# Gated cross-attention and expert layer: attention programs written out for all batches on five engines, in place of a loop on four

## The chip, the cores and the metric

One NeuronCore of a Trainium2 chip runs the whole kernel. The metric is the device time of one execution in microseconds (us); the median of several runs counts. The profile is of one more execution, taken by the hardware profiler.

## The reference

Sixteen batches of 512 tokens with 256 channels. A causal attention with 16 heads of 16 channels (queries from the normalized x, keys and values from a context; only the first 512 context rows can be seen under the causal mask) is added to x through a gate, and a layer of 8 experts, each of which picks its 128 best tokens of a batch, is added through another.

```python
q = _layernorm(x) @ Wq.T;  k = ctx @ Wk.T;  v = ctx @ Wv.T
scores = einsum('bhqd,bhkd->bhqk', q, k) * SCALE
probs = softmax(where(causal, scores, -inf))
x = x + tanh(g_xattn) * (einsum('bhqk,bhkd->bqhd', probs, v) @ Wo.T + bo)
affinity = softmax(_layernorm(x) @ gate_w.T);  gating, idx = top_k(affinity, 128)
h = silu(x_in @ w_gate.T) * (x_in @ w_up.T);  out.at[idx].add(gating * (h @ w_down.T))
x = x + tanh(g_ffn) * out
```

## The kernel before

The program has two stages. `attention` goes through the 16 batches, `experts` through the 8 experts with tokens gathered from memory. The change touches the first alone.

**Passes.** The attention stage is a software pipeline written by hand. `steps(body)` returns the list of steps of one pass. A pass b works on several batches at once: the maxima of the scores and the first score groups of batch b, the other score groups and the values of batch b - 1, the output and second norm of b - 1 and b - 2, and the loads, splits and projections of b + 1 and b + 2. There are passes from -1 to 17; those whose batch would be out of range drop these steps. Each engine (SyncE, TensorE, ScalarE, VectorE, GpSimd) walks the same list and does its own part of each step, so the order of work on each engine is the order of this table.

**Steps that matter below.** "max" (L459 on TensorE, L687 on VectorE) makes the plain scores and their row maxima. "mt" and "mt+" (L501, L585, L694) turn the maxima and write them, negated and in two bf16 parts, to `m_sb`. "mrow" (L399, SyncE) sends `m_sb` as two more rows into the stacked queries `qs`, two small transfers a group. "sc" (L476, L479) makes the score products that need those rows, and ScalarE takes their exponential (L571); "pv" (L493) multiplies with the values. "xturn" and "cturn" (L363) are SyncE's transposing transfers of the split x and context, two each; "qstack" and "kstack" (L383) load the stacked queries and keys of a group from memory, three transfers each; "yturn" (L370) transposes the attention's output. "load" (L335, L337) fetches the next batch. All these transfers are issued by SyncE, in the order of the table.

**Loop and straight code.** `rounds` writes passes -1, 0, 1 and 2 out, then puts the steps of passes 3 to 13 into one loop (`eng.Fori(3, BATCH - 2)`, line 299), and writes 14 to 17 out. SyncE, TensorE, ScalarE and GpSimd use it. VectorE uses `rounds_apart`, which writes all passes out. In the loop the pass number lies in a register, and so does every value that a step waits for:

```python
def count(b, per, k):
    return b * per + k
def wait(eng, s, value):
    if not isinstance(value, int) or value > 0:
        eng.wait_ge(s, value)
def wait_apart(eng, s, value, passed):
    wait(eng, s, value)
    if not isinstance(value, int):
        eng.sem_inc(passed, 1)
```

So a step in the loop computes its value with register operations first, and `wait_apart` makes the wait an instruction of its own that also counts up `passed`. With a constant the value stands in the instruction, and a negative one or zero leaves the wait out. Line 152 of the profile is `eng.wait_ge`, line 160 the `sem_inc`. Inside the loop the DMA addresses come from registers too.

The experts stage has a loop of its own (line 976, `Fori(1, EXPERTS // 2 - 1)`, two rounds of two experts each), unchanged.

Of the kernel before, what the change touches and what calls it, by code (L numbers as in the profile page):

```python
# [13 lines left out]
BATCH = 16  # L14
# [65 lines left out]
def steps(body):  # L80


    b = body
    order = []


    extra = {
        0: {0: [("mrow", b - 1, 3)],
            1: [("ln1+", b + 1, 0), ("yt+", b - 1, 0), ("pv", b - 1, 1, 0), ("yt", b - 1, 0)],
            2: [("xsplit", b + 1, 0)],  # L90
            3: [("mt", b - 1, 3), ("ln1+", b + 1, 1), ("xturn", b + 1), ("xsplit", b + 1, 1), ("pv", b - 1, 1, 1), ("pv", b - 1, 1, 2)],
            4: [("csplit", b + 1, 0), ("o", b - 2, 0, 0), ("o", b - 2, 0, 1), ("mt+", b - 1, 3)],
            5: [("cturn", b + 1)],
            6: [("o+", b - 2, 0), ("o", b - 2, 1, 0)],
            7: [("csplit", b + 1, 1), ("o", b - 2, 1, 1), ("pv+", b - 1, 1), ("pv", b - 1, 1, 3), ("o+", b - 2, 1)],
            9: [("yt", b - 1, 1)]},
        1: {0: [("qstack", b, 2), ("kstack", b, 2)],
            1: [("yturn", b - 1, 0), ("yt+", b - 1, 1), ("mrow", b, 0), ("ysplit", b - 1, 0)],
            2: [("mt", b, 0), ("mt+", b, 0), ("ln2", b - 2, 0)],
            3: [("ln2", b - 2, 1), ("pv", b - 1, 2, 0), ("q", b + 1, 0, 0)],  # L100
            4: [("q+", b + 1, 0), ("q", b + 1, 0, 1), ("q", b + 1, 1, 0)],
            5: [("pv", b - 1, 2, 1)],
            6: [("q", b + 1, 1, 1), ("kstack", b, 3), ("q+", b + 1, 1)],
            8: [("k", b + 1, 0, 0), ("ln2+", b - 2, 1), ("pv", b - 1, 2, 2)],
            9: [("xs", b - 2), ("ln2+", b - 2, 0), ("pv", b - 1, 2, 3)]},
        2: {1: [("pv+", b - 1, 2), ("k+", b + 1, 0), ("k", b + 1, 0, 1)],
            2: [("mt", b, 1), ("mt+", b, 1)],
            3: [("load", b + 2), ("pv", b - 1, 3, 0)],
            4: [("k", b + 1, 1, 0), ("k", b + 1, 1, 1), ("k+", b + 1, 1)],
            5: [("qstack", b, 3), ("yt", b - 1, 2), ("yt+", b - 1, 2), ("pv", b - 1, 3, 1)],  # L110
            7: [("pv", b - 1, 3, 2), ("qstore", b + 1), ("vaug", b)],
            8: [("pv+", b - 1, 3), ("mrow", b, 1), ("pv", b - 1, 3, 3), ("xt", b - 2, 0), ("xt+", b - 2, 0)],
            9: [("res", b - 1), ("xt+", b - 2, 1)],
            10: [("xt", b - 2, 1)]},
        3: {0: [("kstore", b + 1)],
            1: [("mt+", b, 2), ("yt", b - 1, 3), ("yt+", b - 1, 3), ("qstack", b + 1, 0), ("mt", b, 2)],
            3: [("ll+", b - 2), ("pv", b, 0, 0), ("ll", b - 2), ("v", b + 1, 0, 0), ("kstack", b + 1, 0)],
            4: [("v+", b + 1, 0), ("v", b + 1, 0, 1), ("ln1", b + 2, 0), ("mrow", b, 2)],
            5: [("ysplit", b - 1, 1), ("save", b - 2), ("lt", b - 2), ("yturn", b - 1, 1)],
            6: [("kstack", b + 1, 1), ("v", b + 1, 1, 0), ("lt+", b - 2)],  # L120
            8: [("v", b + 1, 1, 1), ("pv", b, 0, 1), ("v+", b + 1, 1)],
            9: [("pv+", b, 0)],
            10: [("ln1", b + 2, 1), ("pv", b, 0, 2), ("qstack", b + 1, 1), ("pv", b, 0, 3)]},
    }
    for g in range(GROUPS):
        sc = (b, g - 2) if g >= 2 else (b - 1, g + 2)
        for k in range(NMAX):
            order.append(("max", b, g, k))
            if k < NSC:
                order.append(("sc", *sc, k))  # L130
            order += extra[g].get(k, [])
    return [p for p in order if not isinstance(p[1], int) or 0 <= p[1] < BATCH]
# [30 lines left out]
def flamingo(nc, x, ctx_kv, g_xattn, g_ffn, wq, wk, wv, wo, bo, gate_w, w_gate, w_up, w_down, out):  # L163
    with ExitStack() as stack:
        def sem(name):
            return stack.enter_context(nc.semaphore(name))

        def sb(ctx, name, shape, dt):
            return ctx.enter_context(nc.sbuf_tensor(name, shape, dt))

        bank = [stack.enter_context(nc.psum_tensor(f"bank{i}", [P, 512], F32)) for i in range(8)]
        max_bank, sc_bank, pv_bank, job_bank = bank[0:3], bank[3:5], bank[5], bank[6:8]


        q_dram = nc.dram_tensor("q_parts", [BATCH, GROUPS, 3, HD * GH, T], BF16, kind="Internal").ap()
        k_dram = nc.dram_tensor("k_parts", [BATCH, GROUPS, 3, HD * GH, T], BF16, kind="Internal").ap()
        tok_dram = nc.dram_tensor("tokens", [BATCH * T, 2 * D], BF16, kind="Internal").ap()

        ident = sb(stack, "ident", [P, P], F32)
        aff = sb(stack, "aff", [P, NT, BATCH * EXPERTS], F32)  # L180
        tanh_g = sb(stack, "tanh_g", [P, 2], F32)
        passed = {n: sem(f"passed_{n}") for n in ("dve", "pool", "sp")}

        with ExitStack() as ctx:
            attention(nc, ctx, stack, sb, sem, locals())
        with ExitStack() as ctx:
            experts(nc, ctx, sb, sem, locals())


def attention(nc, ctx, stack, sb, sem, g):  # L190
# [100 lines left out]
    lmax_done, lexp_done, lsum_done, lrec_done, aff_done = (  # L291
        sem(n) for n in ("lmax_done", "lexp_done", "lsum_done", "lrec_done", "aff_done"))

    def rounds(eng, body):

        for b in (-1, 0, 1, 2):
            for p in steps(b):
                body(b, p)
        with eng.Fori(3, BATCH - 2) as b:
            for p in steps(b):  # L300
                body(b, p)
        for b in range(BATCH - 2, BATCH + 2):
            for p in steps(b):
                body(b, p)

    def rounds_apart(body):

        for b in range(-1, BATCH + 2):
            for p in steps(b):
                body(b, p)  # L310
# [15 lines left out]
    with nc.Block() as block:  # L326
        @block.sync
        def _(sp):
# [85 lines left out]
            for n in ("wq", "wk", "wv", "wo"):  # L414
                load_weights(n)
            sp.dma_start(gw_raw[:, :], g["gate_w"]).then_inc(w_loaded["gate_w"], 16)
            rounds(sp, piece)
            sp.wait_ge(x1_stored, 16 * BATCH)
            sp.wait_ge(tok_stored, 16 * BATCH)

        @block.tensor
        def _(pe):
# [19 lines left out]
            def piece(body, p):  # L442
# [106 lines left out]
                elif kind == "lt":  # L549
                    wait(pe, read["ll"], count(b, 1, 1))  # L550
                    nc.tensor.transpose(to[:, 0:P], llT[:, :], ident[:, :]).then_inc(filled[kind], 1)

            rounds(pe, piece)

        @block.scalar
        def _(act):
# [91 lines left out]
            def later(body, p):  # L648
                if p[0] == "ln1+" and isinstance(p[1], int) and p[1] == 0:
                    return  # L650
                piece(body, p)

            rounds(act, later)

        @block.vector
        def _(dve):
# [112 lines left out]
            dve.wait_ge(tanh_done, 1)  # L769
            nc.vector.tensor_scalar(bias[:, :], bo_rep[:, :], tanh_g[:, 0:1], None, ALU.mult).then_inc(bias_done, 1)  # L770

            rounds_apart(piece)

        @block.gpsimd
        def _(pool):
# [101 lines left out]
                                    base=-1 - SUB * (STACK + 1), pattern=[[0, NT], [-1, P]], channel_multiplier=SUB)\  # L877
                .then_inc(tails_made, 1)
            piece(-1, ("ln1", 0, 1))
            rounds(pool, piece)  # L880


def experts(nc, ctx, sb, sem, g):
# [369 lines left out]
```

## Time and profile before

| | |
|---|---|
| median of 3 runs | 1872.76 us (1872.36 to 1877.73) |
| the profiled execution, its own time | 1872.91 us |
| its span, first to last instruction | 1871.2 us |
| TensorE busy | 1745.9 us (93%) |
| VectorE busy | 1075.4 us (57%) |
| ScalarE busy | 932.2 us (50%) |
| GpSimd busy | 931.7 us (50%) |
| mean granted TensorE clock | 0.974 of full speed |

The 1.7 us between time and span lie around the instructions. "Busy" leaves out register, branch, semaphore and DMA-issuing instructions. A busy TensorE isn't one at its peak, since matmuls are pipelined. The attention stage fills the span up to about 770 us, then the best tokens are sorted out, and the experts fill the rest from about 850 us on.

In what follows a pass of the attention stage is cut at TensorE's first "max" product of the pass: pass 2 is 129.0 to 175.5 us, pass 3 is 175.5 to 222.7, passes 4 to 13 are 222.7 to 675.2, pass 14 is 675.2 to 722.1. PE is TensorE's matmuls, PEld its weight loads; a q behind an engine's name (PEldq, SPq) is its sequencer or its DMA issues.

### The profile page before, as it was taken

The numbers are of one execution on the slowest core, as the hardware profiler recorded it, in microseconds if no ns is written. First come the engines' busy times: TensorE is split into PE (matmuls) and PEld (weight loads), VectorE is DVE, ScalarE is ACT, GpSimd is POOL, SyncE is SP. The second block draws the span as 40 slices with busy tenths as digits, with TensorE's granted clock in tenths as the row PEclk, the third lists the DMA queues.
The fourth block names the chain that finished last, engine by engine and source line by source line (L and its number), as shares of the span: only waits on it lengthen the run. The fifth ranks groups of instructions, "written<-read, shape, count | busy, mean of one in ns | idle before, by whom it ended". The sixth has DMA issues, their size and how long they took to land.

```text
span 1871.2 us, 40632 instructions
## 1 busy us (share of the span) xinstructions
PE 1745.9 (93%) x12838; PEld 1026.6 (55%) x12902; DVE 1075.4 (57%) x3480; ACT 932.2 (50%) x1812; POOL 931.7 (50%) x1026
## 2 busy tenths in 40 slices
PE   4899999999999999818999999999899999999997
PEld 1455555555555555413656565656556565656565
DVE  3788888888888888466443434343343434343421
ACT  2467777777777776523343434343343434343332
POOL 6377788777778885551332324242323232424222
PEclk8899999999999999959999999999999999999999
DMA  6767777778777786365654545656636455555221
GB/s 168 161 172 197 191 199 194 197 197 200 199 196 193 199 199 151 86 162 147 129 103 85 104 85 105 130 78 124 106 67 112 94 96 105 86 96 82 46 32 23
DMA packets 408333, 247.85 MB, mean 132 GB/s; under 512 B 289303, under 2 KB 389759, under 8 KB 408191
## 3 DMA queue, kind: packets, MB, share of 16 engines
q1 hardware_dynamic: 383183, 212.39, 49.4%
q0 software_dynamic: 24576, 33.57, 11.2%
q8 instruction: 72, 1.18, 0.3%
q14 instruction: 70, 0.57, 0.1%
q10 hardware_dynamic: 432, 0.13, 0.0%
HBM read 118.63 MB, written 58.72 MB: 95 GB/s over the span
## 4 chain that ended last, share of the span: by engine, by line
PE 51%; DVE 3%; issue 1%; DMA 1%; ACT 0%; POOL 0%; POOLq 0%; DVEq 0%
PE bank L1108 11%; PE bank L1107 11%; PE bank L1109 11%; PE bank L1125 6%; PE bank L1123 6%; PE bank L1124 6%; DVE h L1225 0%; DVE top_at L1175 0%; DVE h L1228 0%; ACT h L1153 0%; DVE work L1178 0%; DVE top L1173 0%; DMA rows<-tokens,row_now 0%; DMA out<-y,row_now 0%; DMA tokT<-rows 0%
## 5 line engine op out<-in xcount | busy, mean ns | idle before, releaser
L1073 POOL DMA_INDIRECT out<-y,row_now x128 | 202.0, 1578 | 605.9 <-ACT y L1160 581.3
L687 DVE CUSTOM_DVE_ANT_0 masked<-bank,causal 128x128 bf16<-128x128 f32 (+3 forms) x1024 | 449.6, 485 | 62.1 <-PE bank L459 60.0
L571 ACT ACTIVATE prob<-bank 128x512 f32<-128x512 f32 x640 | 360.1, 595 | 140.4 <-PE bank L479 103.1
L1225 DVE TENSOR_TENSOR h<-bank,silu 128x512 f32<-128x512 f32 x256 | 176.4, 689 | 392.5 <-PE bank L1109 258.6
L1153 ACT ACTIVATE h<-h 128x512 bf16<-128x512 f32 x256 | 161.2, 630 | 346.2 <-DVE h L1225 324.5
L1228 DVE TENSOR_TENSOR h<-h 128x512 bf16<-128x512 f32 x256 | 177.4, 693 | 179.4 <-ACT h L1153 171.8
L1125 PE MATMUL bank<-downT,h 128*128 128x256 bf16 x1024 | 279.1, 273 | 0.0
L1124 PE MATMUL bank<-downT,h 128*128 128x256 bf16 x1024 | 279.1, 273 | 0.0
L1123 PE MATMUL bank<-downT,h 128*128 128x256 bf16 x1024 | 279.1, 273 | 0.0
L459 PE MATMUL bank<-ks,qs 96*128 96x128 bf16 (+3 forms) x1024 | 254.9, 306 | 19.2 <-DMA ks<-k_parts 10.2
L1108 PE MATMUL bank<-tokT,gateT 128*128 128x512 bf16 x511 | 194.7, 381 | 35.4 <-DMA tokT<-rows 28.9
L476 PE MATMUL bank<-qs,ks 128*128 128x128 bf16 x1024 | 200.0, 221 | 12.8 <-DMA qs<-m_sb 9.1
L1107 PE MATMUL bank<-tokT,upT 128*128 128x512 bf16 x511 | 194.6, 381 | 6.7 <-DVE h L1225 6.6
L479 PE MATMUL bank<-qs,ks 98*128 98x384 bf16 (+2 forms) x768 | 196.7, 274 | 0.0
L1108 PE MATMUL bank<-tokT,upT 128*128 128x512 bf16 x512 | 194.6, 380 | 0.1
L1109 PE MATMUL bank<-tokT,upT 128*128 128x512 bf16 x512 | 194.6, 380 | 0.0
L840 POOL TENSOR_SCALAR_AFFINE_SELECT prob<-prob 128x512 f32<-128x512 f32 x256 | 156.4, 637 | 72.7 <-ACT prob L571 72.5
L493 PE MATMUL bank<-prob,v_aug 128*32 128x512 f32 (+3 forms) x2048 | 185.8, 447 | 2.9 <-ACT yT L579 2.9
L1107 PE MATMUL bank<-tokT,gateT 128*128 128x512 bf16 x481 | 182.8, 380 | 2.5 <-ACT silu L1147 0.9
L1160 ACT ACTIVATE y<-bank,gate_now 128x256 f32<-128x256 f32 x128 | 53.7, 471 | 260.7 <-PE bank L1125 260.7
L1109 PE MATMUL bank<-tokT,gateT 128*128 128x512 bf16 x481 | 183.3, 381 | 0.1
L1060 POOL DMA_INDIRECT rows<-tokens,row_now x128 | 130.1, 1016 | 92.6 <-DVE row_now L1216 54.8
(141 smaller groups left out, 2675.4 us busy)
## 6 DMA issues: line engine op xcount, KB each, us to landing
q_parts<-q_sb SPq DMA_DIRECT2D x64, 192.0 KB, 4.5
k_parts<-k_sb SPq DMA_DIRECT2D x64, 192.0 KB, 3.8
qs<-q_parts SPq DMA_DIRECT2D x64, 192.0 KB, 3.5
ks<-k_parts SPq DMA_DIRECT2D x64, 192.0 KB, 3.1
x_t<-in_x SPq DMA_DIRECT2D x16, 512.0 KB, 4.2
ctx_t<-in_ctx SPq DMA_DIRECT2D x16, 512.0 KB, 5.5
qs<-q_parts SPq DMA_DIRECT2D x64, 128.0 KB, 3.3
ks<-k_parts SPq DMA_DIRECT2D x64, 128.0 KB, 3.0
```

Of the source, the lines that this page charges most:

```text
L459: last = nc.tensor.matmul(dst[:, h * w:(h + 1) * w], qs[0:STACK, gr, h0 + h, i * P:(i + 1) * P], ks[0:STACK, gr, h0 + h, 0:w], start=True, ...
L476: last = nc.tensor.matmul(dst[:, at:at + P], ks[:, gr, h0 + h, j * P:(j + 1) * P], qs[:, gr, h0 + h, j * P:(j + 1) * P], start=True, stop= ...
L479: last = nc.tensor.matmul(dst[:, at + P:at + PWIDTH[j]], ks[0:ROWS, gr, h0 + h, j * P:(j + 1) * P], qs[0:ROWS, gr, h0 + h, (j + 1) * P:T], ...
L571: nc.scalar.activation(prob[:, gr % 2, h0:h0 + nh, POFF[tiles[0]]:POFF[tiles[0]] + w], sc_bank[SC_BANK[k]][:, 0:nh * w].rearrange("p (h w) ...
L687: last = nc.vector.tensor_tensor_reduce(masked[:, (gr * NMAX + k) % 2, part], max_bank[max_at(gr, k)][:, part], causal[:, T - w:T], 1.0, L ...
L1073: nc.gpsimd.indirect_dma_start(out_rows, bass.IndirectOffsetOnAxis(ap=row_now[:, par, c, s:s + 1], axis=0), y[:, c % 2, s, :], None, compu ...
L1107: nc.tensor.matmul(banks[it % 2][:, :], hi, xh, start=(dh == 0), stop=False)
L1108: nc.tensor.matmul(banks[it % 2][:, :], hi, xl, start=False, stop=False)
L1109: last = nc.tensor.matmul(banks[it % 2][:, :], lo, xh, start=False, stop=(dh == NH2 - 1))
L1123: nc.tensor.matmul(to, hh, wh, start=(it == 0), stop=False)
L1124: nc.tensor.matmul(to, hh, wl, start=False, stop=False)
L1125: last = nc.tensor.matmul(to, hl, wh, start=False, stop=(it == IT - 1))
```

## The change

`rounds` loses its loop and becomes what `rounds_apart` was: passes -1 to 17 one after the other, with the pass number a constant. All five engines use it. The order of the steps in a pass is the same.

```diff
--- before.py
+++ after.py
@@ -291,19 +291,7 @@
     lmax_done, lexp_done, lsum_done, lrec_done, aff_done = (
         sem(n) for n in ("lmax_done", "lexp_done", "lsum_done", "lrec_done", "aff_done"))
 
-    def rounds(eng, body):
-
-        for b in (-1, 0, 1, 2):
-            for p in steps(b):
-                body(b, p)
-        with eng.Fori(3, BATCH - 2) as b:
-            for p in steps(b):
-                body(b, p)
-        for b in range(BATCH - 2, BATCH + 2):
-            for p in steps(b):
-                body(b, p)
-
-    def rounds_apart(body):
+    def rounds(body):
 
         for b in range(-1, BATCH + 2):
             for p in steps(b):
@@ -414,7 +402,7 @@
             for n in ("wq", "wk", "wv", "wo"):
                 load_weights(n)
             sp.dma_start(gw_raw[:, :], g["gate_w"]).then_inc(w_loaded["gate_w"], 16)
-            rounds(sp, piece)
+            rounds(piece)
             sp.wait_ge(x1_stored, 16 * BATCH)
             sp.wait_ge(tok_stored, 16 * BATCH)
 
@@ -550,7 +538,7 @@
                     wait(pe, read["ll"], count(b, 1, 1))
                     nc.tensor.transpose(to[:, 0:P], llT[:, :], ident[:, :]).then_inc(filled[kind], 1)
 
-            rounds(pe, piece)
+            rounds(piece)
 
         @block.scalar
         def _(act):
@@ -650,7 +638,7 @@
                     return
                 piece(body, p)
 
-            rounds(act, later)
+            rounds(later)
 
         @block.vector
         def _(dve):
@@ -769,7 +757,7 @@
             dve.wait_ge(tanh_done, 1)
             nc.vector.tensor_scalar(bias[:, :], bo_rep[:, :], tanh_g[:, 0:1], None, ALU.mult).then_inc(bias_done, 1)
 
-            rounds_apart(piece)
+            rounds(piece)
 
         @block.gpsimd
         def _(pool):
@@ -877,7 +865,7 @@
                                     base=-1 - SUB * (STACK + 1), pattern=[[0, NT], [-1, P]], channel_multiplier=SUB)\
                 .then_inc(tails_made, 1)
             piece(-1, ("ln1", 0, 1))
-            rounds(pool, piece)
+            rounds(piece)
 
 
 def experts(nc, ctx, sb, sem, g):
```

On TensorE, where pass 3 begins. Before, this is the start of the loop (`bank` is a PSUM bank, `qs` and `ks` the stacked queries and keys, `ISA` and `REGISTER_ALU` are register operations):

```order
L299 ISA
L152 ISA [waits stack_loaded0]
L459 MATMUL bank<-ks,qs 128x128 [waits max_read]
L459 MATMUL bank<-ks,qs 128x128 x3
L152 ISA
L152 ISA [waits mrow_loaded2]
L476 MATMUL bank<-qs,ks 128x128 [waits exp_done]
L479 MATMUL bank<-qs,ks 128x384
L459 MATMUL bank<-ks,qs 128x256 [waits max_read]
L459 MATMUL bank<-ks,qs 128x256
L152 REGISTER_ALU
```

The same place with the change:

```order
L447 MATMUL bank<-ks,qs 128x128 [waits max_read,stack_loaded0]
L447 MATMUL bank<-ks,qs 128x128 x3
L464 MATMUL bank<-qs,ks 128x128 [waits exp_done,mrow_loaded2]
L467 MATMUL bank<-qs,ks 128x384
L447 MATMUL bank<-ks,qs 128x256 [waits max_read]
L447 MATMUL bank<-ks,qs 128x256
L464 MATMUL bank<-qs,ks 128x128 [waits exp_done]
L467 MATMUL bank<-qs,ks 128x256
```

The products and their order are the same; the register operations in front of them are gone, and two waits that stood apart are now in the products they belong to. Where pass 3 ends there was a branch; now the products of pass 4 follow.

On SyncE, where pass 3 begins, the transfers on the way to the first group's maxima. Before (start of the loop; `xT` and `cT` are the transposed x and context):

```order
L299 ISA
L152 REGISTER_ALU [waits mt_read]
L399 DMA qs<-m_sb 1x16x128 [waits sc_filled]
L399 DMA qs<-m_sb 1x16x128
L152 ISA
L363 DMA_TRANSPOSE xT<-x_nat 128x8x128 [waits x_lo_split,q_filled]
L363 DMA_TRANSPOSE xT<-x_nat 128x8x128
L363 DMA_TRANSPOSE cT<-c_nat 128x8x128 [waits c_lo_split,v_filled]
L363 DMA_TRANSPOSE cT<-c_nat 128x8x128
L152 ISA
L152 ISA [waits q_stored]
L383 ISA [waits sc_filled]
```

With the change:

```order
L387 DMA qs<-m_sb 1x16x128 [waits sc_filled,mt_read]
L387 DMA qs<-m_sb 1x16x128
L351 DMA_TRANSPOSE xT<-x_nat 128x8x128 [waits q_filled,x_lo_split]
L351 DMA_TRANSPOSE xT<-x_nat 128x8x128
L351 DMA_TRANSPOSE cT<-c_nat 128x8x128 [waits v_filled,c_lo_split]
L351 DMA_TRANSPOSE cT<-c_nat 128x8x128
L371 DMA qs<-q_parts 48x2048 [waits sc_filled,q_stored]
L371 DMA qs<-q_parts 32x2048
```

The transfers stand in the same order, with no register operations between them. Lines moved up by 12 with the deleted function. As a whole TensorE's program has 8553 rows where it had 6261 (rows group instructions, and a loop's rows stand once), SyncE's 939 instead of 513, ScalarE's 1526 instead of 1058, GpSimd's 874 instead of 470, and VectorE's 3338 as before.

## Rows read from the trace of the kernel before

**Rows 1.** Page, part 1: busy us (share), instructions.

```profile
PE 1745.9 (93%) x12838; PEld 1026.6 (55%) x12902; DVE 1075.4 (57%) x3480; ACT 932.2 (50%) x1812; POOL 931.7 (50%) x1026
```

**Rows 2.** Line 299 (the passes' loop): count, ns min/median/max, first and last start.

```profile
L299 PEldq COMPARE_BRANCH  x11: 76/208/235, 222.0 to 674.5; - x11
...
L299 PEldq MOVE  x1: 29/29/29, 174.7 to 174.7; - x1
```

**Rows 3.** Stretches: us, busy (x) by engine, PEclk, DMA, GB/s; passes 2, 3, 14.

```profile
129.00:175.50 46.50, 44.79 (x426) 25.98 (x422) 39.10 (x170) 33.27 (x66) 36.25 (x47) 1.00 0.72 184
175.50:222.70 47.20, 44.97 (x426) 26.13 (x422) 39.25 (x170) 33.36 (x66) 36.05 (x47) 1.00 0.75 183
675.20:722.10 46.90, 45.04 (x426) 25.98 (x423) 38.52 (x168) 33.27 (x66) 36.35 (x47) 1.00 0.84 182
```

**Rows 4.** The same, last line: passes 4 to 13 together.

```profile
sum 452.50, PE 448.10 PEld 261.44 DVE 389.41 ACT 331.99 POOL 360.70; mean PE 44.81 PEld 26.14 DVE 38.94 ACT 33.20 POOL 36.07
```

**Rows 5.** Line 152 (waits), stretch 358.4 to 403.7, one loop pass.

```profile
L152 PEldq ALU_OP  x97: 32/32/36, 358.8 to 401.8; - x97
...
L152 PEldq EVENT_SEMAPHORE  x18: 51/51/51, 359.2 to 398.4; - x18
...
L152 PEldq FUSED_REGOPS  x17: 37/37/65, 358.9 to 403.7; - x17
```

**Rows 6.** DMA queues, passes 4 to 13: packets, MB, share.

```profile
q1 hardware_dynamic: 120661, 89.66, 79.0%
q14 instruction: 18, 0.15, 0.1%
```

**Rows 7.** DMA queues, pass 14.

```profile
q8 instruction: 4, 0.07, 0.6%
q14 instruction: 4, 0.03, 0.2%
```

**Rows 8.** DMA queues, pass 2.

```profile
q8 instruction: 3, 0.05, 0.5%
q14 instruction: 4, 0.03, 0.3%
```

**Rows 9.** Waits, pass 2: us, times, longest.

```profile
PE bank L476 <- DMA qs<-m_sb: 1.7, 1, 1.7
```

**Rows 10.** Waits, pass 3.

```profile
PE bank L476 <- DMA qs<-m_sb: 1.7, 2, 0.9
```

**Rows 11.** Waits, pass 14.

```profile
PE bank L476 <- DMA qs<-m_sb: 1.6, 1, 1.6
```

**Rows 12.** Waits, passes 4 to 13.

```profile
PE bank L476 <- DMA qs<-m_sb: 1.8, 5, 0.6
```

**Rows 13.** Timeline, SyncE issues in pass 13: start, us.

```profile
642.70 2.62 SPq L363 DMA_TRANSPOSE cT<-c_nat  x2
...
647.36 1.32 SPq L383 DMA_DIRECT2D ks<-k_parts  x3
```

**Rows 14.** The same in pass 3.

```profile
188.46 3.73 SPq L363 DMA_TRANSPOSE cT<-c_nat  x2
```

**Rows 15.** DMA queues, 189.5 to 191.2 us.

```profile
q8 instruction: 1, 0.02, 5.0%
```

**Rows 16.** The SyncE issues in pass 14.

```profile
692.24 1.97 SPq L383 DMA_DIRECT2D ks<-k_parts  x3
```

**Rows 17.** DMA queues, 692.0 to 693.5 us.

```profile
q8 instruction: 1, 0.02, 4.4%
```

**Rows 18.** Timeline, TensorE in pass 14: start, us, idle before.

```profile
700.23 0.23 PE L476 MATMUL bank<-qs,ks 128*128 128x128 bf16 x1 [1.55 <-DMA qs<-m_sb]
```

**Rows 19.** Line 976 (the experts' loop).

```profile
L976 PEldq COMPARE_BRANCH  x2: 76/3070/6063, 1340.7 to 1597.1; - x2
```

**Rows 20.** Timeline, TensorE at the experts' back edge.

```profile
1347.62 0.63 PE L1108 MATMUL bank<-tokT,gateT 128*128 128x512 bf16 x1 [4.96 <-issue]
```

## The prediction

> **What bounds the kernel now.** I read the page's busy times first: TensorE has work for 1745.9 us [rows 1] of the 1871.2 us span, far ahead of every other engine. Then I cut the attention stage into passes. Line 299 is the loop that holds passes 3 to 13 on TensorE: it is entered at 174.7, its branch runs first at 222.0 and last, the eleventh time, at 674.5 [rows 2]. Ten passes (4 to 13) thus take 452.5 us, 45.25 us each. In the stretches, TensorE is busy for 448.1 of these 452.5 us [rows 4], so only 4.4 us of gaps are left in ten passes, back edges included. A loop pass is TensorE's own work and hardly anything else. That is the first thing to see: **the loop has next to nothing to give back**.
>
> The second is that the passes that are already written out are the longer ones. Pass 2 takes 46.5 us and pass 14 takes 46.9; pass 3, the first time through the loop's code, takes 47.2. All three have the same matmuls (x426) and full clock (PEclk 1.00) [rows 3]. Against 45.25 that is 1.25, 1.65 and 1.95 us more.
>
> The third is where the excess lies. In each of the three, TensorE waits 1.6 to 1.7 us for the transfer qs<-m_sb [rows 9 to 11]; in ten loop passes together it waits 1.8 us for it [rows 12]. In pass 14 it is one hole of 1.55 us, at 700.23 [rows 18]: the first score product (L476) of a group needs the row of negated maxima. That small transfer stands in SyncE's queue behind the two cT transposes, six stack loads and one yT transpose.
>
> The fourth is what differs. The q8 and q14 instruction queues carry program code. In passes 4 to 13 there are 18 packets on q14 and none on q8 [rows 6]; in pass 14 alone there are 4 on each [rows 7], in pass 2 there are 3 and 4 [rows 8]. So TensorE, ScalarE, GpSimd and SyncE find a loop's code still at hand, and only VectorE, written out already, keeps loading (18 packets in ten passes). The size 0.07 MB over 4 is about 16 KB a block on q8, 8 KB on q14. Where such a block falls into the chain of transfers, SyncE's issues drag: the pair of cT transposes takes 2.62 us to issue in pass 13 [rows 13], and 3.73 us in pass 3 [rows 14], with one q8 block between 189.5 and 191.2 [rows 15]. The three ks loads take 1.32 us in pass 13 [rows 13] and 1.97 us in pass 14 [rows 16], with one q8 block between 692.0 and 693.5 [rows 17].
>
> **The change, part by part.**
>
> *Register arithmetic goes.* In one loop pass TensorE's sequencer runs 97 ALU_OPs of 32 ns and 17 FUSED_REGOPS of 37 ns [rows 5], 3.7 us in all, beside 45 us of matmuls that it runs ahead of. What hides it is the queue of matmuls; had it cost time, it would stand in the 4.4 us of gaps. Gain between 0 and 4.4 us over the ten passes. I take 0, since the written-out passes, which have none of it, aren't shorter. For SyncE, ScalarE and GpSimd the same: their operations of this kind end in a wait for TensorE's pace, and what they could save lies in the same 4.4 us.
>
> *Extra wait instructions go* (the waits that also count up the semaphore "passed"). Bound and value are the same 0 to 4.4 us, counted once.
>
> *Ten back edges go.* TensorE's takes 208 ns at the median [rows 2], inside the sequencer's lead. Value 0; bounds again in the 4.4 us.
>
> *Code must now be loaded in every pass.* This is the term that counts. A pass of TensorE is some 426 matmuls and 422 weight loads [rows 3] plus about 20 waits, near 870 instructions; pass 14 loaded 4 blocks for them and pass 2 loaded 3. Ten passes so add some 34 blocks on q8 and about 20 on q14. Their bytes are nothing (0.07 MB in a pass against 8 to 9 MB); it is their place that costs. The nearest rows are the three passes that do load: 1.25, 1.65 and 1.95 us. Ten passes at these prices are 12.5, 16.5 and 19.5 us. From below the bound is 0, should the blocks fall beside the chain; from above I take the dearest pass, 19.5 us, and a little over. I choose 1.3 us a pass, near the cheapest of the three, because a block comes every 13 us (45 us over 3.4) and only a part of the pass is sensitive: in pass 13, which starts at 629.9, it runs from the issue of the cT pair at 642.70 [rows 13] to about where pass 14 has its hole, 25 us after a start at 675.2 [rows 3, 18]. Some 12 us of 45, by this estimate, so some passes will be missed. **+13 us.**
>
> *Pass 3 itself* (47.2 us) already loads its code, and passes 1, 2, 14 and later are untouched. 0, within 1 us either way.
>
> *The experts stage* isn't changed, but its code moves. TensorE's back edge at line 976 holds it for up to 6063 ns [rows 19], and TensorE idles 4.96 us there [rows 20]. Where the target lies may change what that branch costs: between 5 us less and 5 us more. I take 0.
>
> The sum is made against the profiled execution: 1872.91 + 13 = **1886 us**. That execution is 0.15 us above the median of the three runs (1872.76), so it serves for both. About 0.3% (5.6 us) is what a measurement of this kernel can tell from no change.
>
> The Trainium skill, "Runtime: NRT & Kernel Launch", section "Instruction fetch mechanics", speaks against my term: it says that the sequencer fetches the next block while the current one runs, and that crossing a block is mostly hidden. By it the sum would be 1872.9. The written-out passes disagree, not because TensorE starved for code, but because other transfers came late.
>
> **The rivals.**
>
> *The loads are hidden (chance 0.18).* Then passes 2, 3 and 14 are long for reasons of their own: pass 2 stands near the start, pass 3 carries the entry into the loop, pass 14 is the first after it. For it: three passes are few. Against it: all three show the same wait of 1.6 to 1.7 us, which the ten others have at 0.18 us in the mean and 0.6 at the longest [rows 12]. Time 1872.9, or down to 1872.9 - 4.4 = 1868.5 if all gaps close too.
>
> *The loads cost more (0.13).* Not only SyncE's issues but ScalarE's or GpSimd's own code comes late, in passes whose blocks meet both the first and the second group's chain, as pass 3 (two waits [rows 10]). At 2.2 us a pass the change costs 22 us, 1895; it decides if the mean of passes 4 to 13 goes over 47.2.
>
> *Faster: the back edges were dear (0.04).* The place is TensorE's branch. If each of ten cost what the experts' one costs, 4.96 us [rows 20], the time would be 1872.9 - 49.6 = 1823. But 4.4 us of gaps in ten passes exclude nearly all of it. What is left: all gaps closed, and the experts' loop lands better, 1872.9 - 4.4 - 5.0 = 1863.5. It decides from 5.6 us on, so it needs both. The same section of the Trainium skill states this rule (a taken branch out of the resident window waits for a fetch, hence a preference for full unrolling); the trace agrees at the experts' back edge and not at this loop's, where the branch takes 208 ns.
>
> *The change doesn't do what it says* has no room here: the order of the work in a pass is the same in both programs.
>
> **How the numbers follow.** Forecast 0.65 at 1886 us. The range reaches down to the hidden case, 1873, and up to the dear one, 1895; below 1873 and above 1895 I leave about 2 in 10. Slower by over 0.3% (above 1878.5): the forecast and the dear case, 0.77, the two summing to 0.78 with a little off for a forecast that comes out small. Within 0.3%: the hidden case and that little, 0.19. Faster: 0.04.
>
> **What would show it.** Right: in passes 4 to 13 of the new profile q8 carries 3 or 4 packets a pass, about 34, and q14 some 38 in place of 18; these passes average 46 to 47 us; the waits of L476 for qs<-m_sb grow from 1.8 us to 8 or more; the line-152 ALU_OPs are gone from the attention stage; TensorE's matmul times and PEclk stay. Wrong: q8 packets in each pass and yet passes of 45.3 us (then hidden), or passes of 45.3 us with a different total (then the experts' back edge moved), or passes under 44.9 us, which would say that register work did hold TensorE up.

## The result and the profile after

| | before | with the change |
|---|---|---|
| median of 12 runs each | 1873.72 us (1872.36 to 1878.44) | 1881.07 us (1878.10 to 1885.80) |
| ratio, 95% interval | 1 | 1.0037 (1.0027 to 1.0047) |
| the profiled execution, its span | 1872.91, 1871.2 us | 1884.75, 1883.0 us |

The change makes the kernel 7 us slower, 0.37%. The profiled execution of the changed kernel is one of its slower ones, 3.7 us above the median, so the profile shows 11.8 us of difference where the medians show 7.4.

Page, part 1, of the changed kernel (compare [rows 1]):

```profile
PE 1752.6 (93%) x12838; PEld 1026.7 (55%) x12902; DVE 1075.8 (57%) x3480; ACT 934.3 (50%) x1812; POOL 933.0 (50%) x1026
```

The stretches of the changed kernel, cut into passes as before (columns as in [rows 3]): pass 3, passes 4 to 13 together, then passes 4, 9, 10 and 12 alone, and pass 14.

```profile
174.00:222.40 48.40, 46.54 (x426) 26.54 (x423) 39.16 (x170) 33.65 (x66) 36.28 (x47) 0.96 0.85 189
222.40:683.70 461.30, 451.75 (x4214) 260.98 (x4211) 390.20 (x1691) 333.22 (x660) 361.52 (x461) 0.99 0.81 195
222.40:267.30 44.90, 44.79 (x425) 25.98 (x421) 38.85 (x170) 33.25 (x66) 36.05 (x47) 1.00 0.80 193
450.50:498.60 48.10, 46.45 (x426) 26.52 (x423) 39.25 (x170) 33.55 (x66) 36.30 (x47) 0.96 0.79 185
498.60:547.30 48.70, 46.53 (x425) 26.58 (x421) 39.10 (x170) 33.63 (x66) 36.22 (x47) 0.96 0.87 190
593.50:638.50 45.00, 44.76 (x426) 25.98 (x423) 38.90 (x170) 33.23 (x66) 36.08 (x47) 1.00 0.81 199
683.70:733.90 50.20, 47.66 (x425) 26.92 (x422) 38.54 (x168) 33.76 (x66) 36.28 (x47) 0.93 0.75 169
```

Passes 4 to 13 take 461.3 us against 452.5 [rows 4], 8.8 us more. Pass 4 and pass 12 are as short as any loop pass; pass 9 and pass 10 are 3 us longer. Pass 14 was already written out and is 3.3 us longer too (50.2 against 46.9). Pass 3 is 1.2 us longer (48.4 against 47.2), and what comes ahead of it is shorter by 1.5, so pass 4 begins within 0.3 us of where it did; everything after pass 14 takes the same 1149.1 us. And another column moves: the granted clock, 1.00 in all of [rows 3], is 0.96 in passes 3, 9 and 10 and 0.93 in pass 14.

The DMA queues in passes 4 to 13 (compare [rows 6]):

```profile
q8 instruction: 34, 0.56, 0.5%
q14 instruction: 34, 0.28, 0.2%
```

34 blocks on q8 where there were none, 34 on q14 where there were 18. The waits of TensorE in the same ten passes (compare [rows 12]):

```profile
PE bank L464 <- DMA qs<-m_sb: 7.2, 8, 1.6
...
PE bank L447 <- DMA ks<-k_parts: 0.8, 2, 0.7
```

The wait of the score product for its maxima has grown from 1.8 to 7.2 us, and a wait for the stacked keys has come up. The deepest hole, in pass 14 (compare [rows 18]), with what SyncE issued ahead of it (compare [rows 16]):

```profile
709.34 0.29 PE L464 MATMUL bank<-qs,ks 128*128 128x128 bf16 x1 [2.45 <-DMA qs<-m_sb]
```

```profile
699.05 1.72 SPq L371 DMA_DIRECT2D qs<-q_parts  x3
700.87 1.30 SPq L371 DMA_DIRECT2D ks<-k_parts  x3
...
703.95 1.17 SPq L387 DMA_DIRECT2D qs<-m_sb  x2
```

The clock adds a second price to the same holes. TensorE's timeline after the hole of pass 10, and the granted clock (PEclk, third column from the right) of three short stretches there:

```profile
521.97 0.40 PE L447 MATMUL bank<-ks,qs 96*128 96x128 bf16 x4 [0.67 <-DMA ks<-k_parts]
523.82 0.23 PE L464 MATMUL bank<-qs,ks 128*128 128x128 bf16 x1 [1.45 <-DMA qs<-m_sb]
...
525.02 1.49 PE L510 MATMUL bank<-cT,wkT 128*128 128x512 bf16 x3
...
529.25 1.46 PE L510 MATMUL bank<-cT,wkT 128*128 128x512 bf16 x6
```

```profile
524.00:526.00 2.00, 2.00 (x10) 1.08 (x8) 0.78 (x4) 1.34 (x3) 1.91 (x2) 0.50 1.07 273
526.00:527.50 1.50, 1.50 (x8) 0.80 (x7) 0.33 (x1) 1.05 (x3) 1.00 (x1) 0.55 1.15 369
527.50:531.00 3.50, 3.50 (x28) 1.61 (x26) 2.27 (x10) 1.96 (x5) 1.77 (x2) 1.00 1.05 268
```

TensorE stood still for 0.67 and 1.45 us, with four products between. Then it ran at half clock (0.50, the lower of its two levels, 1.2 GHz) until about 527.3: three of the products of L510 take 1.49 us, six take 1.46 at full clock behind it. Such a stretch is 3.4 us long in passes 3, 9 and 10, at 199.7, 476.1 and 523.9 us, and 6.8 us in pass 14, at 708.2; half of it is lost. Of the 6.8 us in pass 14 the first 1.1 us still lie in the hole, in which no product runs. In passes 2 to 14 of all profiles of this study, each drop to half clock begins in a hole before score products or within about 1 us after one. That splits the 8.8 us of passes 4 to 13 into 5.4 us more waiting for m_sb (7.2 less 1.8), 0.8 us for the keys, and 3.4 us of clock (two stretches of 3.4 us, half of each): 9.6 us, a little over what is to be explained.

Register work is indeed gone. Line 152 on TensorE in pass 7 (compare [rows 5], 97 ALU_OPs and 17 FUSED_REGOPS, now none):

```profile
L152 PEldq EVENT_SEMAPHORE  x32: 51/51/51, 359.3 to 404.3; - x32
```

### The profile page after: what moved, and what is told of

Same layout as the page of the kernel before. It is cut to its first block, busy times and chain, and to the rows that moved or that the text cites. A ratio compares the mean times of both kernels' runs of the same rounds, so it can differ in the third digit from the quotient of the medians.

```text
span 1883.0 us, 37315 instructions
## 1 busy us (share of the span) xinstructions
PE 1752.6 (93%) x12838; PEld 1026.7 (55%) x12902; DVE 1075.8 (57%) x3480; ACT 934.3 (50%) x1812; POOL 933.0 (50%) x1026
## 4 chain that ended last, share of the span: by engine, by line
PE 51%; DVE 3%; DMA 1%; issue 1%; ACT 0%; POOL 0%; POOLq 0%; DVEq 0%
PE bank L1096 11%; PE bank L1095 11%; PE bank L1097 11%; PE bank L1113 6%; PE bank L1111 6%; PE bank L1112 6%; DVE h L1213 0%; DVE top_at L1163 0%; DVE h L1216 0%; ACT h L1141 0%; DVE work L1166 0%; DVE top L1161 0%; DMA rows<-tokens,row_now 0%; DMA tokT<-rows 0%; DMA out<-y,row_now 0%
```

## The experiments

Theory A: TensorE's 16 KB code blocks make SyncE's chain of transfers late. Rival B: it is the code of the three other engines, or their constants. All times are medians; "before" is the kernel before, run on the same chip in the same rounds.

### One part of the change at a time

TensorE alone written out:

```diff
-            rounds(pe, piece)
+            rounds_apart(piece)
```

> The kernel before, with TensorE's attention program alone written out; SyncE, ScalarE and GpSimd keep the loop. Theory A (TensorE's 16 KB code blocks fall into SyncE's chain of transfers and make them late): q8 carries about 33 packets in passes 4 to 13, q14 stays near 18, and most of the loss of the full change is here: 5 to 8 us over before, about 1880. Rival B (it is the code of SyncE, ScalarE and GpSimd, in 8 KB blocks, or their waits and issues in constant form): no more than 1 us over before, 1873 to 1875. If both share it: 3 to 4 us over.

Measured: 1887.91 us against 1873.46, ratio 1.0078 (1.0060 to 1.0096): **14.5 us slower, twice the full change.** Its ten passes take 465.3 us, 12.8 more than before:

```profile
q8 instruction: 34, 0.56, 0.5%
q14 instruction: 18, 0.15, 0.1%
```

```profile
PE bank L476 <- DMA qs<-m_sb: 9.7, 10, 1.6
...
PE bank L459 <- DMA ks<-k_parts: 1.7, 3, 0.9
...
PE bank L522 <- DMA xT<-x_nat: 1.0, 2, 0.7
```

The whole cost belongs to TensorE's code, as theory A has it, but the size was missed, 14.5 us for an expected 5 to 8: something else in the full change gives 7 us back. The opposite half, with TensorE alone in the loop and the others written out (`rounds_loop` is the old `rounds`):

```diff
         @block.tensor
...
-            rounds(piece)
+            rounds_loop(pe, piece)
```

> The changed kernel, with TensorE alone put back into the loop; SyncE, ScalarE, GpSimd and VectorE are written out. q8 is empty in passes 4 to 13, q14 carries about 33. Theory A: within 1.5 us of before, 1873 to 1875. Rival B: all of the loss stays, about 1880 to 1881. Together with the run before it: if A and B add, the two excesses sum to about 7 to 8 us.

Measured: 1874.75 us, ratio 1.0008 (0.9994 to 1.0022), no difference that can be told. In passes 4 to 13 (221.2 to 677.0 us) q14 carries its 34 packets and q8 none:

```profile
q14 instruction: 34, 0.28, 0.2%
PE bank L476 <- DMA qs<-m_sb: 4.1, 9, 1.7
```

So B, which wanted 1880 to 1881, is out. The 8 KB blocks are not quite free, though: TensorE's wait for m_sb grows from 1.8 to 4.1 us and these ten passes take 455.8 us, 3.3 more than before, most of it in pass 9, which takes 48.1 us with a hole of 1.66 us and 3.4 us at half clock behind it. What happens there is read in the next section. But the two halves do not add: 14.5 and 1.3 make 7.4. Writing out the three other engines gains nothing while TensorE loops and 7 us when it doesn't. SyncE's issues show what it can be. Pass 7 starts at 358.4 in the kernel before and at 358.6 in the changed one. Before:

```profile
371.23 2.61 SPq L363 DMA_TRANSPOSE cT<-c_nat  x2
374.36 1.27 SPq L383 DMA_DIRECT2D qs<-q_parts  x3
375.88 1.32 SPq L383 DMA_DIRECT2D ks<-k_parts  x3
377.48 1.25 SPq L370 DMA_TRANSPOSE ynT<-y_nat  x1
379.09 1.18 SPq L399 DMA_DIRECT2D qs<-m_sb  x2
```

With the change:

```profile
371.09 2.60 SPq L351 DMA_TRANSPOSE cT<-c_nat  x2
373.79 1.45 SPq L371 DMA_DIRECT2D qs<-q_parts  x3
375.34 1.29 SPq L371 DMA_DIRECT2D ks<-k_parts  x3
376.73 1.24 SPq L358 DMA_TRANSPOSE ynT<-y_nat  x1
378.07 1.23 SPq L387 DMA_DIRECT2D qs<-m_sb  x2
```

The issues themselves take about the same time; the gaps between them, in which the loop's SyncE computes addresses and values, are gone. From the end of the cT pair to the start of the m_sb pair it was 5.25 us (379.09 less 373.84) and is 4.38 (378.07 less 373.69). The m_sb pair starts 19.5 us into the pass instead of 20.7. Two more kernels tell whether this is what pays. SyncE written out with TensorE:

```diff
-            rounds(sp, piece)
+            rounds_apart(piece)
...
-            rounds(pe, piece)
+            rounds_apart(piece)
```

> The kernel before with TensorE and SyncE written out (and VectorE, as before); ScalarE and GpSimd keep the loop. TensorE alone written out cost 14.5 us where the full change costs 7. Theory: SyncE's constants give the difference back, since it then issues the first group's m_sb transfers about 1.1 us earlier in a pass (19.5 in place of 20.7 us): 1879 to 1883. Rival (ScalarE or GpSimd give it back, or the difference is chance): 1885 to 1889.

Measured: 1879.03 us against 1873.61, ratio 1.0031 (1.0017 to 1.0044). And its complement, TensorE, ScalarE and GpSimd written out, SyncE in the loop:

```diff
-            rounds(pe, piece)
+            rounds_apart(piece)
...
-            rounds(act, later)
+            rounds_apart(later)
...
-            rounds(pool, piece)
+            rounds_apart(piece)
```

> The complement: TensorE, ScalarE and GpSimd written out, SyncE in the loop. Theory (SyncE's constants give it back): without them the cost stays at that of TensorE alone, 1885 to 1890, and the m_sb transfers are issued at about 20.7 us of a pass or later. Rival (ScalarE or GpSimd): 1879 to 1883.

Measured: 1886.10 us, ratio 1.0065 (1.0047 to 1.0083). Both as the theory said. In passes 4 to 13 the first group's m_sb pair is issued 19.7 to 21.3 us into a pass with SyncE written out, 20.5 to 21.7 with SyncE in the loop. The waits in passes 4 to 13, first with SyncE written out, then with SyncE in the loop (the second profile is of the slowest of its six executions, 7.5 us above their median, so it overstates the difference):

```profile
PE bank L476 <- DMA qs<-m_sb: 6.1, 7, 1.4
```

```profile
PE bank L476 <- DMA qs<-m_sb: 12.9, 13, 2.0
```

It is SyncE's straight code, without the register work, that gives back more than half of what TensorE's costs (1887.91 to 1879.03). ScalarE and GpSimd matter little: with their programs written out as well, 1887.91 becomes 1886.10 and 1879.03 becomes 1881.07.

### Room in the chain

If the blocks cost only by making the m_sb transfers late, then room ahead of these transfers must take the cost away. The m_sb pair of the first group waits for nothing but its place in SyncE's queue: VectorE writes it about 5 us before SyncE issues it. In pass 13 of the kernel before, the two are (VectorE's timeline, SyncE's timeline):

```profile
645.22 0.27 DVE L694 SCALAR_TENSOR_TENSOR m_sb<-bank,m_sb 16x128 bf16<-16x128 f32 x1
```

```profile
650.57 1.18 SPq L399 DMA_DIRECT2D qs<-m_sb  x2
```

In the table of steps, "mrow" goes ahead of "yturn":

```diff
-            1: [("yturn", b - 1, 0), ("yt+", b - 1, 1), ("mrow", b, 0), ("ysplit", b - 1, 0)],
+            1: [("mrow", b, 0), ("yturn", b - 1, 0), ("yt+", b - 1, 1), ("ysplit", b - 1, 0)],
```

In the kernel before:

> The kernel before, with the first group's two small m_sb transfers (mrow) issued by SyncE ahead of the yT transpose instead of behind it, nothing else. They are issued about 1.3 us earlier, and no longer wait for that transpose to land. Theory (the chain cT, stacks, yT, m_sb ends last before the first score product): the holes of 0.2 to 0.8 us there vanish, 1 to 4 us faster than before, 1869 to 1873. Rival (the stack loads or VectorE's maxima end last there): no change.

Measured: 1868.91 us against 1873.46, ratio 0.9977 (0.9966 to 0.9988), 4.5 us faster, a little over the 1 to 4 expected. In the changed kernel:

> The changed kernel with the same one step moved (m_sb transfers ahead of the yT transpose). Theory: the loss sits in the hole before the first group's score product, which now has a microsecond or more to spare, so it recovers more than the same move does in the kernel before: 5 to 9 us faster than the changed kernel, 1872 to 1876. Rival 1 (TensorE itself waits for its code, or the loss is spread over other waits): it stays at 1879 to 1881. Rival 2 (the move only helps as much as in the kernel before): 1 to 4 us faster, 1877 to 1880.

Measured: 1872.11 us, ratio to before 0.9995 (0.9979 to 1.0010), so 9.0 us under the changed kernel's 1881.07. The same move is worth twice as much where code is loaded. The second group has the same shape one step further on: its "mrow" stands behind "qstore", four stores of 192 KB. With that pair moved as well:

```diff
-            7: [("pv", b - 1, 3, 2), ("qstore", b + 1), ("vaug", b)],
-            8: [("pv+", b - 1, 3), ("mrow", b, 1), ("pv", b - 1, 3, 3), ("xt", b - 2, 0), ("xt+", b - 2, 0)],
+            7: [("pv", b - 1, 3, 2), ("mrow", b, 1), ("qstore", b + 1), ("vaug", b)],
+            8: [("pv+", b - 1, 3), ("pv", b - 1, 3, 3), ("xt", b - 2, 0), ("xt+", b - 2, 0)],
```

> The kernel before with the first group's m_sb transfers ahead of the yT transpose, as in the run that gained 4.5 us, and the second group's ahead of the q stores too. Theory (the holes of 0.4 to 0.9 us before the second group's score product, at 34 to 36 us of a pass, come from these transfers standing behind four stores): 1 to 3 us faster than with the first move alone, 1866 to 1868. Rival (the stores are then late and hold up the next pass's stacks): 1869 to 1875.

Measured: 1862.89 us against 1873.61, ratio 0.9942 (0.9925 to 0.9958). That is 6 us beyond the first move, where 1 to 3 were expected. In passes 4 to 13 one wait of 0.2 us is left:

```profile
PE bank L476 <- DMA qs<-m_sb: 0.2, 1, 0.2
```

These passes take 449.4 us, 2.5 us less than with the first move (451.9). Most of the rest of the gain lies ahead of them: pass 4 begins at 213.5 us where it began at 219.2. Of these 5.7 us, 4.1 lie in passes 1 to 3, which are written out; the other 1.6 lie before pass 1, where the profiles of kernels that are the same up to there differ by as much.

Both moves in the changed kernel:

> The changed kernel with both groups' m_sb transfers moved ahead (of the yT transpose, and of the q stores). Theory (the code blocks cost only by making these two chains late): with room in both, the loss of 7 us all but vanishes against the loop kernel with the same two moves (1862.9): 1863 to 1867, and passes 4 to 13 under 453 us. Rival (a part of the loss is elsewhere, as late stacks or TensorE's own code): 1868 to 1872.

Measured: 1863.05 us against 1872.97, ratio 0.9945 (0.9926 to 0.9964). **The loss of 7 us is gone**, as far as medians with intervals of some 3 us to each side can tell: with both moves, loop and straight code stand at 1862.89 and 1863.05. The blocks still come, and in passes 4 to 13 no wait for m_sb is left at all; what is left is the stacked keys:

```profile
q8 instruction: 34, 0.56, 0.5%
```

```profile
PE bank L447 <- DMA ks<-k_parts: 1.6, 3, 1.0
```

```profile
213.90:665.50 451.60, 447.92 (x4214) 259.91 (x4210) 389.57 (x1691) 331.77 (x660) 360.59 (x461) 1.00 0.83 201
```

Ten passes in 451.6 us at full clock: 9.7 us under the changed kernel, and 2.2 over the loop kernel with the same moves. So the profiles still show a small price, most of it the wait for the keys. Last, TensorE in the loop, the others written out, with both moves:

> TensorE in the loop, the other four written out, with both moves: no 16 KB blocks in passes 4 to 13, and SyncE issues without register work. Theory: the loop on TensorE is what matters, and with both chains short SyncE's constants have nothing left to give: 1861 to 1864, the same as the loop kernel with both moves. Rival 1 (SyncE's constants help once more): 1858 to 1860. Rival 2 (the 8 KB blocks of three more engines cost by themselves): 1866 to 1870.

Measured: 1860.43 us, ratio 0.9927 (0.9909 to 0.9946), the fastest kernel of this study, 12.5 us under before. It falls between the theory's 1861 to 1864 and rival 1's 1858 to 1860, and the 2.5 us to the loop kernel lie inside the intervals of the two, so which of them holds is open; rival 2 is out.

### Where the blocks begin

The block boundaries fall at other instructions if TensorE's code is shifted. Three kernels do that with semaphore increments that nobody waits for. The first puts 128 at the start of TensorE's program:

```diff
         @block.tensor
         def _(pe):
+            shifted = sem("shifted")
+            for _ in range(128):
+                pe.sem_inc(shifted, 1)
             pe.wait_ge(consts, CONSTS)
```

> The changed kernel with 128 extra semaphore increments at the start of TensorE's program, which shift its later code by half a 16 KB block; TensorE has idle time there. Theory (the blocks come all the time, and which passes they hit changes, but not how many): the total stays within 3 us of the changed kernel, 1878 to 1884, with other passes long. Rival (one unlucky alignment makes the whole loss): back near 1873, or past 1887.

Measured: 1894.37 us against 1873.61, ratio 1.0104 (1.0083 to 1.0124). The total is past the rival's 1887, but the experiment was badly placed. TensorE has no idle time there: its first transposes start at 20.56 us, not at 9.76, and pass 4 begins at 233.0 us, not at 222.4. The passes themselves, 4 to 13, take 463.9 us, near the changed kernel's 461.3. The other two put fewer increments ahead of the first score product, where TensorE waits 9.5 us for its stacks:

```diff
                     if k == 0:
+                        if b == 0 and gr == 0:
+                            for _ in range(104):
+                                pe.sem_inc(shifted, 1)
                         wait(pe, stack_loaded[gr], count(b, 96, 96))
```

> The changed kernel with 104 semaphore increments in TensorE's program, now just ahead of its first score product, where it waits 9.5 us for the first stacks anyway. They take about 80 ns each by the start that the earlier 128 cost (10.8 us), 8.3 us, so they should be free. All later TensorE code shifts by 104 instructions against the blocks of 256. Theory (blocks come in every pass, wherever they begin): 1878 to 1884, passes 4 to 13 at 458 to 465 us. Rival (the alignment of the blocks sets the cost): below 1876 or above 1887, with passes 4 to 13 outside 456 to 467.

> The same with 56 increments, 4.5 us, in the same place: a second alignment. Theory: 1878 to 1884 again. Rival: another total, outside 1876 to 1887, or 4 us and more from the run with 104.

Measured: 1887.92 us (ratio 1.0069, 1.0053 to 1.0086) with 104, 1883.12 us (1.0047, 1.0030 to 1.0064) with 56. The 104 were not free either: the first product comes at 48.2 us instead of 42.8. The total with 56 is inside the theory's 1878 to 1884; the one with 104 misses it, is past the rival's 1887, and the two lie 4.8 us apart, where the rival wanted 4 or more. In passes 4 to 13 the four alignments (0, 56, 104, 128) take 461.3, 466.0, 462.5 and 463.9 us, all well over the loop's 452.5 and inside the 456 to 467 beyond which the rival would have held. So the loss is no accident of one alignment, but its size is not the same for all, and which passes are long does change: 9 and 10 in the changed kernel, 9 and 4 with 128, 9 and 7 with 104, 7 and 12 with 56. With 56 increments the ten passes cost most and the total is the lowest of the three shifted ones; in its profile pass 4 begins 4 us earlier than in the changed kernel's. Each of these is one profiled execution, and the executions of one kernel differ by several microseconds (1878.10 to 1885.80 for the changed one).

## Why the prediction was right, and where it was off

*What bounds the kernel.* The bound, the chain and its end were read correctly: the loss is in the passes that now load code, mostly at the wait for qs<-m_sb, and the two moves that give this chain room take away all of it that medians can tell. Two of the signs named did not come as stated: the wait grew to 7.2 us, not to 8 or more, and the granted clock did not stay.

*Ten back edges.* No gain from them shows, as taken: with room in the chain, loop and straight code are equal within the intervals (1862.89 and 1863.05).

*Code in every pass.* 34 blocks on q8 were forecast and 34 came; on q14 it was 34 for a forecast of some 38. The price of 1.3 us a pass is what TensorE's code costs alone: 12.8 us in ten passes in the profile of e1_tensore_out, 14.5 us in the medians. **The term was sized right, for a kernel that isn't this one**, and in part by luck: 1.7 us of the 12.8 is half clock (3.4 us of it, from 523.4), which the prediction did not reckon with.

*Register arithmetic goes.* This is the step that failed. I bounded its gain by the 4.4 us of gaps in the loop's passes and took 0, "since the written-out passes, which have none of it, aren't shorter". That bound holds only where nothing else changes. SyncE's register work lies ahead of the m_sb transfers, and once the blocks make these late, it counts: 14.5 us with SyncE in the loop and TensorE out become 5.4 us with SyncE written out too. Nor did SyncE's operations end in a wait for TensorE's pace, as the prediction had it: at the m_sb transfers it was TensorE that waited for SyncE's chain. The two terms had to be priced together. The sum was 13 - 0; measured it is 14.5 - 7, so the forecast of 1886 came out 5 us too high.

*The nearest rows.* Passes 2, 3 and 14 load code, but SyncE has constants in 2 and 14 and registers in 3, and I read one price from all three. Pass 3, the dearest at 1.95 us, was the only one with register work on SyncE, and I didn't weigh that. Whether this made it the dearest is not shown: with SyncE written out it takes 46.6 us in one kernel (e2_tensore_loop) and 48.4 in the changed one.

*The clock* was expected to stay. The written-out passes ran at full clock in [rows 3], although pass 14 had a hole of 1.55 us. In the changed kernel such holes bring half clock for 3.4 or 6.8 us. With it, by an estimate from these rows, a hole of 1.45 us costs 3.2 us (half of 3.4 on top) and the one of 2.45 us costs 5.3 (half of the 5.7 us at half clock that lie behind it).

*The rivals.* That the loads are hidden is refuted by e1_tensore_out. The Trainium skill ("Runtime: NRT & Kernel Launch", section "Instruction fetch mechanics") states that crossing a code block is mostly hidden. For the engine that executes the code the traces here agree: a wait of TensorE for its own code shows in no row of the passes. The cost falls on other engines' transfers, which that section does not speak of. The dear case, 22 us or more, was reached by no kernel. The faster case did not come; the experts' back edge moved from 6063 to 5599 ns, and what follows pass 14 took 1149.1 us both times.

*How a block makes the chain late.* The prediction saw SyncE's issues stretch [rows 13 to 17]. That happens, but it is only a part. In pass 9 of the changed kernel the m_sb pair is issued 19.7 us into the pass, a microsecond earlier than in the loop; it is the transfers that stay under way longer. Below are a code block, if there is one, then the second cT transpose and the m_sb pair with their microseconds from issue to landing (last number). Pass 4 of the changed kernel (44.9 us long):

```profile
cT<-c_nat SPq DMA_TRANSPOSE x1, 3.2
qs<-m_sb SPq DMA_DIRECT2D x2, 4.0 KB, 2.3
```

Pass 9 of the same kernel (48.0 us), with a q14 block 15.3 us into the pass:

```profile
q14 instruction: 1, 0.01, 1.0%
cT<-c_nat SPq DMA_TRANSPOSE x1, 4.0
qs<-m_sb SPq DMA_DIRECT2D x2, 4.0 KB, 4.3
```

And pass 10 (48.7 us), with a q8 block 15.7 us into it:

```profile
q8 instruction: 1, 0.02, 2.3%
cT<-c_nat SPq DMA_TRANSPOSE x1, 4.7
```

The traces of the nine kernels without a moved step agree, over passes 2 to 14. In the 76 passes in which no block begins between 14.0 and 16.4 us, the second cT transpose lands 3.1 to 3.5 us after its issue. In the 37 in which one begins between 14.2 and 16.1 us, while that transpose is being issued or is under way, it takes 3.8 to 5.6 us, whichever queue the block came on. (In the four with a block at 16.3 or 16.4 us it takes 3.2 to 5.2 us.) The stacks, the yT transpose and the m_sb pair land behind it. In the changed kernel passes 8, 9 and 10 have such a block and average 47.6 us, the other seven of the ten 45.5. These are passes of one kernel with the same code, so the difference goes with the block and not with the other form of the waits. The shifted kernels say the same: their long passes (9 and 4, 9 and 7, 7 and 12) are ones with a block 15.0 to 16.3 us into the pass. Not every such pass is long, and a second block can add to the first: pass 9, with the q14 block at 15.3 to 15.6 us alone, takes 45.3 to 45.6 us in the kernel before, e1_tensore_out and e5_tensore_synce_out; in the changed kernel and e2_tensore_loop, where another q14 block comes at 22.1 or 22.4 us, while the m_sb pair is under way, it takes 48.0 and 48.1. *Still open* is why a block of 8 or 16 KB holds up the transfers around it, and the holes of passes without a block in this place, such as the 1.07 us of pass 7, are not explained by it.

## What to carry over

Writing a loop out is not free when its body fits where the engine keeps its code: look at the instruction queues in the passes of each kind, and at which chain of transfers has no room. Look also at when in a pass the blocks come: in the changed kernel each of the ten passes loads blocks, and they take from 44.9 to 48.7 us. Try an unrolling engine by engine; here TensorE gained nothing from it and paid, and SyncE, whose register work stood ahead of a critical transfer, gained once TensorE's blocks had made that transfer late. Before changing how code is laid out, look for a small transfer that is ready long before it is issued: moving two of them in SyncE's order gave 10.7 us, more than the whole question of loop or straight code.

## What was not expected of the hardware

- TensorE's 16 KB blocks, 34 in ten passes and 0.5% of the DMA time, cost 14.5 us through the transfers of another engine; the 8 KB blocks of three engines cost nothing that the medians could tell (1.3 us, interval -1.1 to +4.1), though one pass of ten was 3 us longer.
- A block that began 14.2 to 16.1 us into a pass came with a transpose that took 3.8 to 5.6 us to land in place of 3.1 to 3.5, a block of 8 KB as well as one of 16 KB.
- Holes of 0.67 and 1.45 us close together in a dense TensorE stream were followed by 3.4 us at 1.2 GHz. A hole of 1.55 us in the kernel before [rows 18], 0.25 us of idling 2 us ahead of it, was not, nor was one of 2.12 us in pass 9 of e12_shift_56. The size of the hole alone doesn't tell.
- Semaphore increments on TensorE cost some 84 ns each when nothing hides them (10.8 us for 128).
- TensorE's back edge over the loop of 11 passes takes 208 ns; over the larger body of the experts it takes between 5.3 and 7.1 us in the kernels of this study, and it idles most of that.
